# One batch's last tiles in two orders: TensorE's and VectorE's own, two transposes copied by ScalarE, and routing logits computed without a transpose

## The reference, cut to what matters

```python
x = x + attn(layernorm(x))        # 16 heads of 16; rotated scores over a plain-score denominator
x = x + ffn(layernorm(x))
# ffn(x):
out_shared = square(relu(x @ Ws1)) @ Ws2
logits = x @ Wr                                   # 8 experts
top_vals, top_idx = top_k(logits, 2)
prob = trunc(scatter(softmax(top_vals), top_idx)) # is 1 only where one softmax weight rounds to 1
out = out_shared + sum_e prob[e] * (square(relu(x @ W1[e])) @ W2[e])
```

## Time and profile before

| | |
|---|---|
| time, median of 3 runs | 1656.57 us (1656.44 to 1657.23) |
| the profiled execution's own time | 1656.43 us |
| its span | 1654.7 us |
| ScalarE busy | 1587.1 us, 96% of the span |
| TensorE busy | 1483.4 us, 90% |
| last score exponential ends | 1625.3 us; 29 us of the span follow it |

### The profile page before, as it was taken

One profiled execution on the slowest core, in us unless ns is written; L12 is line 12 of the kernel. 1 busy time (PEld: TensorE's weight loads), 2 busy tenths in 40 slices (PEclk: granted clock), 3 DMA queues, 4 the chain that ended last, 5 costly groups with the idle time before them and its releaser, 6 DMA issues.

```text
span 1654.7 us, 25505 instructions
## 1 busy us (share of the span) xinstructions
PE 1483.4 (90%) x8226; PEld 572.7 (35%) x8226; DVE 851.1 (51%) x1961; ACT 1587.1 (96%) x2641; POOL 521.9 (32%) x863
## 2 busy tenths in 40 slices
PE   4888989999999989999899899989999999999986
PEld 2322333333333333333343343333333333333334
DVE  5334434765346653566445653566434665356416
ACT  2999999999999999999999999999999999999992
POOL 3324133432234322333332323334133432234310
PEclk8998999999999999999999999999999999999998
DMA  5532233331434313333234234333243421433300
GB/s 160 156 99 80 86 106 115 120 101 55 131 115 131 111 44 122 122 124 106 80 118 124 94 96 131 100 121 97 73 131 115 141 93 42 135 113 103 115 27 26
DMA packets 95389, 172.05 MB, mean 104 GB/s; under 512 B 15696, under 2 KB 82256, under 8 KB 83152
## 3 DMA queue, kind: packets, MB, share of 16 engines
q1 hardware_dynamic: 94656, 169.55, 32.7%
q10 hardware_dynamic: 592, 0.79, 0.2%
HBM read 111.55 MB, written 58.72 MB: 103 GB/s over the span
## 4 chain that ended last, share of the span: by engine, by line
ACT 88%; PE 6%; issue 4%; DVE 1%; DMA 1%; DVEq 0%; ACTq 0%; POOL 0%; SPq 0%; POOLq 0%
ACT scores L541 57%; ACT probs L551 27%; ACT probs L553 4%; PE scores L599 2%; PE y_ps L628 1%; PE side L638 1%; PE scores L606 1%; PE scores L657 0%; DMA x_in<-in_L_attn_x 0%; PE side L657 0%; PE scores L647 0%; PE scores L773 0%; ACTq L315 0%; PE scores L784 0%; DVEq L894 0%
## 5 line engine op out<-in xcount | busy, mean ns | idle before, releaser
L541 ACT ACTIVATE scores<-scores 128x1024 f32<-128x1024 f32 x1024 | 1067.6, 1122 | 16.8 <-PE scores L599 16.5
L599 PE MATMUL scores<-stack 96*128 96x512 bf16 x2048 | 585.3, 385 | 77.8 <-ACT scores L541 40.1
L551 ACT ACTIVATE probs<-scores 128x1024 f32<-128x1024 f32 x512 | 491.7, 1111 | 2.8 <-PE scores L606 1.7
L606 PE MATMUL scores<-stack 96*128 96x512 bf16 (+3 forms) x1536 | 335.0, 330 | 46.7 <-ACT scores L541 37.6
L438 POOL TENSOR_SCALAR_AFFINE_SELECT probs<-probs 128x256 f32<-128x256 f32 (+1 forms) x640 | 240.8, 403 | 387.7 <-ACT probs L551 219.0
L628 PE MATMUL y_ps<-probs,v_sb 128*32 128x512 f32 (+3 forms) x3072 | 331.8, 504 | 5.1 <-POOL probs L438 5.1
L599 PEld LDWEIGHTS scores<-stack 96*128 96x128 bf16 x2048 | 152.6, 97 | 486.1 <-ACT scores L541 209.9
L541 ACT ACTIVATION_READ_ACCUMULATOR scores<-scores 128x1 f32 x1024 | 300.5, 293 | 0.0
L448 POOL TENSOR_TENSOR parts<-rest,parts 128x512 bf16<-128x512 f32 x124 | 143.2, 1155 | 292.8 <-DVE parts L961 292.8
L606 PEld LDWEIGHTS scores<-stack 96*128 96x128 bf16 x1536 | 116.9, 98 | 300.1 <-ACT scores L541 154.5
L446 POOL TENSOR_TENSOR rot<-raw,cos_sb 128x512 f32<-128x512 f32 x62 | 89.3, 1440 | 390.2 <-DVEq L971 390.2
(11 more groups left out here) (141 smaller groups left out, 1062.0 us busy)
## 6 DMA issues: line engine op xcount, KB each, us to landing
stack<-qk_parts SPq DMA_DIRECT2D x756, 128.0 KB, 2.6
qk_parts<-parts SPq DMA_DIRECT2D x127, 384.0 KB, 2.6
out<-x_mid SPq DMA_DIRECT2D x32, 256.0 KB, 2.9
x_in<-in_L_attn_x SPq DMA_DIRECT2D x7, 1024.0 KB, 5.3
stack<-qk_parts SPq DMA_DIRECT2D x18, 64.0 KB, 2.3
x_in<-in_L_attn_x SPq DMA_DIRECT2D x2, 512.0 KB, 4.4
probs<-in_L_attn_Wqkv SPq DMA_DIRECT2D x1, 512.0 KB, 5.7
cos_sb<-in_cos SPq DMA_DIRECT2D x1, 512.0 KB, 6.5
```

What stands on the lines that cost most here:

```text
L541: nc.scalar.activation(src, src, ACT.Exp, scale=SCALE, accum_out=den[:, g % 2, i, j:j + 1]).then_inc(exp_done, 1)
L551: nc.scalar.activation(probs[:, chunk % 2, j, :], src, ACT.Exp, scale=SCALE).then_inc(exp_done, 1)
L599: mm = nc.tensor.matmul(tile[:, half * HALF:(half + 1) * HALF], q[:, j, i * P:(i + 1) * P], k[:, j, half * HALF:(half + 1) * HALF], start= ...
L606: mm = nc.tensor.matmul(tile[:, col:col + n], k[:, h, i * P:(i + 1) * P], q[:, h, q0:q0 + n], start=True, stop=True)
```

## The change

The list is given in two orders. `END_TILES` is the order in which TensorE fills tiles, `END_READ` the one in which VectorE reads them, and `END_COPIED` names two tiles, ("t2", 0) and ("t2", 1), that ScalarE copies to `xn2t` after its last exponential, with a semaphore of its own, `end_copied`. The tiles logits_t are gone: a logits tile is now 4 blocks times 2 halves of the contraction, with the tokens as the stationary operand (128x128) and the 8 router columns as the moving one, and it waits for both t2 tiles of its half. VectorE's read of it is a plain copy of 32 columns. TensorE's waits name the tile (`end_read`) instead of its number. The routed tile now comes before ("down", 0) and ("down", 1).

```diff
-END_TILES = [("norm", 0), ("acc", 2), ("acc", 3), ("t2", 2), ("t2", 3), ("norm", 1), ("up", 2),
-             ("logits_t", 1), ("acc", 0), ("acc", 1), ("up", 3), ("down", 2), ("t2", 0), ("t2", 1),
-             ("logits", 1), ("down", 3), ("logits_t", 0), ("up", 0), ("up", 1), ("logits", 0), ("down", 0),
-             ("down", 1), ("routed", 0)]
+END_TILES = [("norm", 0), ("acc", 2), ("acc", 3), ("t2", 2), ("t2", 3), ("norm", 1), ("acc", 0), ("acc", 1), ("up", 2),
+             ("up", 3), ("logits", 1), ("t2", 0), ("t2", 1), ("down", 2), ("logits", 0), ("up", 0), ("down", 3), ("up", 1),
+             ("routed", 0), ("down", 0), ("down", 1)]
+END_READ = [("norm", 0), ("acc", 2), ("acc", 3), ("t2", 2), ("t2", 3), ("norm", 1), ("acc", 0), ("acc", 1), ("up", 2),
+            ("up", 3), ("logits", 1), ("down", 2), ("logits", 0), ("up", 0), ("routed", 0), ("down", 3), ("up", 1),
+            ("down", 0), ("down", 1)]
+END_COPIED = [("t2", 0), ("t2", 1)]
...
+            for tile in END_COPIED:
+                n, t = END_TILES.index(tile), tile[1]
+                act.wait_ge(end_full, n + 1)
+                nc.scalar.activation(xn2t[:, :, 2 * t * P:(2 * t + 2) * P], bank(n).rearrange("p (k n) -> p k n", k=KC),
+                                     ACT.Copy).then_inc(end_copied, 1)
             exp_gap(B - 1)
...
+            def end_read(tile):
+
+                if tile in END_COPIED:
+                    pe.wait_ge(end_copied, END_COPIED.index(tile) + 1)
+                else:
+                    pe.wait_ge(end_taken, END_READ.index(tile) + 1)
+
...
-                elif what == "logits_t":
-                    pe.wait_ge(end_taken, END_TILES.index(("t2", 2 * t + 1)) + 1)
-                    for k in range(KC):
-                        for j in range(2):
-                            mm = nc.tensor.matmul(side[32 * j:32 * j + 32, 0:2 * P], wr_sb[:, k, :],
-                                                  xn2t[:, k, (4 * t + 2 * j) * P:(4 * t + 2 * j + 2) * P],
-                                                  start=k == 0, stop=k == KC - 1, tile_position=(0, 32 * j),
-                                                  skip_group_check=True)
                 elif what == "logits":
-                    pe.wait_ge(end_taken, END_TILES.index(("logits_t", t)) + 1)
-                    for i in range(2):
-                        mm = nc.tensor.transpose(side[:, i * P:(i + 1) * P], logits_t[:, i * P:(i + 1) * P], ident[:, :])
+                    end_read(("t2", 2 * t))
+                    end_read(("t2", 2 * t + 1))
+                    for i in range(NB // 2):
+                        for k in range(KC):
+                            mm = nc.tensor.matmul(side[:, i * E:(i + 1) * E], xn2t[:, k, (4 * t + i) * P:(4 * t + i + 1) * P],
+                                                  wr_sb[:, k, 0:E], start=k == 0, stop=k == KC - 1)
...
             for n in range(IN_LOOP, len(END_TILES)):
-                pe.wait_ge(end_taken, n - 2 * RING + 1)
+                if n >= 2 * RING:
+                    end_read(END_TILES[n - 2 * RING])
                 end_tile(n, bank(n))
...
-                elif what == "logits_t":
-                    nc.vector.tensor_copy(logits_t[0:P // 2, :], side[0:P // 2, 0:2 * P]).then_inc(end_taken, 1)
                 elif what == "logits":
                     half = slice(t * NB // 2, (t + 1) * NB // 2)
-                    nc.vector.tensor_copy(logits[:, half, :].rearrange("p (j i) e -> p i j e", i=2),
-                                          side[:, 0:2 * P].rearrange("p (i j e) -> p i j e", i=2, j=4)[:, :, 0:2, 0:E]
+                    nc.vector.tensor_copy(logits[:, half, :].rearrange("p i e -> p (i e)"), side[:, 0:E * NB // 2]
                                           ).then_inc(end_taken, 1)
...
-            for n in range(IN_LOOP, len(END_TILES)):
-                end_tile(n, bank(n))
+            for tile in END_READ[IN_LOOP:]:
+                end_tile(tile, bank(END_TILES.index(tile)))
             experts(last_b)
```

More of the change, by code:

```diff
@@ L276, in block @@
         end_taken = sem("end_taken")
+        end_copied = sem("end_copied")
         raw_of = [raw[:, :], y_sb[:, 0, 0:HALF]]
@@ L758, in end_tile @@
                 elif what == "acc":
-                    pe.wait_ge(end_taken, END_TILES.index(("norm", 1 - t // 2)) + 1)
+                    end_read(("norm", 1 - t // 2))
                     for i in range(2):
@@ L768, in end_tile @@
                                                      xn[:, t % 2, i, k * P:(k + 1) * P], ident[:, :])
-                elif what == "logits_t":
-                    pe.wait_ge(end_taken, END_TILES.index(("t2", 2 * t + 1)) + 1)
-                    for k in range(KC):
-                        for j in range(2):
-                            mm = nc.tensor.matmul(side[32 * j:32 * j + 32, 0:2 * P], wr_sb[:, k, :],
-                                                  xn2t[:, k, (4 * t + 2 * j) * P:(4 * t + 2 * j + 2) * P],
-                                                  start=k == 0, stop=k == KC - 1, tile_position=(0, 32 * j),
-                                                  skip_group_check=True)
-                elif what == "logits":
-                    pe.wait_ge(end_taken, END_TILES.index(("logits_t", t)) + 1)
-                    for i in range(2):
-                        mm = nc.tensor.transpose(side[:, i * P:(i + 1) * P], logits_t[:, i * P:(i + 1) * P], ident[:, :])
+                elif what == "logits":
+                    end_read(("t2", 2 * t))
[4 more added lines that the diff above has]
+                                                  wr_sb[:, k, 0:E], start=k == 0, stop=k == KC - 1)
                 elif what == "up":
-                    pe.wait_ge(end_taken, END_TILES.index(("t2", t)) + 1)
+                    end_read(("t2", t))
                     for k in range(KC):
@@ L1096, in ffn_tile, with end_tile @@
                     dve.drain().then_inc(out_ready, 1)
-            def end_tile(n, side):
-                what, t = END_TILES[n]
+            def end_tile(tile, side):
+                what, t = tile
                 b = B - 1
@@ L1105, in end_tile @@
                     route(b)
-                dve.wait_ge(end_full, n + 1)
+                dve.wait_ge(end_full, END_TILES.index(tile) + 1)
                 if what == "norm":
@@ L1220, in batch @@
                         if kind == "end":
-                            end_tile(t, side)
+                            end_tile(END_READ[t], side)
                         elif kind == "v":
```

## The result

The changed kernel takes 1659.88 us (median of 14 executions, 1656.43 to 1662.79) against 1656.51 of the kernel before on the same chip (14, 1654.41 to 1659.59): a ratio of 1.0022 with a 95% interval of 1.0015 to 1.0029. It is slower by 3.4 us, just over the 0.2% that I had set as the bound, and inside the range; but the forecast was "no change, a shade faster", and it is rival 3's time, 1659.7, that came. The profiled execution took 1659.48 with a span of 1657.9.

A forecast was written before the change was run, and what follows sets the result against it. ScalarE's exponentials bound the kernel (88% of the chain), with a 28.3 us tail at stake. Gains of 2.4 + 0.5 less 2.6 given back left 0.3 us: 1656.3 us, range 1653.7 to 1660.0.

The forecast's parts named there:

- rival 3: Second tail stretch: logits 0's small products don't count as work, clock low to the end; 1659.7 us, chance 0.25.
- the sum: Whole tail: clock low at 1637.70, back 6.0 us after restart; 2.4 + 0.5 gained, 2.6 lost, 0.3 left; chance 0.45.
- rival 2: Second tail stretch: clock stays high after short idle; last add 1649.4, span end 1652.1, time 1654.0 us; chance 0.20.
- the end: After the last add: store issue, landing and SyncE's last wait take 2.7 us; span ends 1654.4 against 1654.7.
- acc ahead: First tail part: acc directly behind norm's read, so the first transpose starts at 1637.70; 2.4 us gained.
- hidden behind VectorE's layernorm: TensorE's up 2, up 3 and logits 1 fit beside VectorE's 5.8 us, ending 1635.5 with 2.2 us to spare.
- one of the two things that were to show me wrong: Signs of error: down 2 waiting for hidden 2, or TensorE waiting for ScalarE's copies; neither was expected.
- the price of a small product: Logits tile: each load with 8 columns starts 0.11 us apart at the high clock, 0.22 at the low.
- The upper end: Small products of the logits tile: whole load with nothing overlapped, 0.19 us at the high clock, 0.333 at the low.
- the second half of rival 3: Logits 0 at the low clock with whole 0.333 us loads: 1.8 us more, 1661.5 us; chance 0.10.
- the copies: ScalarE copies two transposed tiles, 598 ns each, no second table load charged; 0.7 us cover before TensorE needs them.
- The rule that transposes don't count as work for the clock: Second tail stretch: 6.0 us would count from down 2, clock rising at 1645.45; 1656.9 us, chance 0.10; rows spoke against it.

The follow-up runs named there:

- the cut kernel: Changed kernel computing 2 of its 8 batches, compared with the kernel before cut likewise: 469.98 us against 466.31.
- the fillers: Unneeded 256-column identity products in TensorE's idle tail stretches, added to the changed kernel (1651.67 us) and to the kernel before (1652.63 us).
- the fifth profile: Changed kernel unaltered, run once more for a profile of its slower group: profiled execution 1661.28 us, span 1659.7.
- the filled one: Changed kernel plus unneeded products on TensorE (4 ahead of norm, 1 behind it, 6 behind logits 1): 1651.67 us, repeated 1652.25.
- the first profile: Changed kernel as first measured, nothing further altered: profiled execution 1659.48 us, span 1657.9.
- the cut kernel before: Kernel before the change computing only 2 of its 8 batches: 466.31 us.
- the third profile: Changed kernel unaltered, run once more for a profile: profiled execution 1656.21 us, span 1654.6.

## Why the prediction failed

- **The mechanism was on the page, the weight was wrong.** The step that failed is the one that sets the sum: "If the clock is low at 1637.70 ... and comes back 6.0 us after the restart, at 1643.7". It treats the return as something that any work earns after six microseconds, the 16 small products of logits 0 included. In four of the five profiles of the full changed kernel the clock was back 2.7 to 4.0 us after the second restart (tails of 27.9, 28.3, 27.7 and 27.1), in the fifth it was low until 12.9 us after it (32.4), and in the cut kernel for ten microseconds (31.6). With wide products ahead of the small ones it was 6.0 again. The sum's middle case was met by none. What the runs showed in its place: when logits 0 runs at the low clock, the clock stays low for 10.2 to 13.7 us in all, and the tail lasts 31.4 to 32.6 us where the kind case has 27.1 to 28.3. The parts taken singly say that the router tile makes the loss, and the times, of which 18 in 26 lie at 1659.5 or above, that a loss is the usual case: rival 3 had 0.25 and should have weighed most. How it acts is seen in four profiles, two of them with VectorE's copies, and agrees with the fillers, which take the whole loss back.
- **How close rival 3 came is in part luck.** By its sum the tail was to last 32.6 us (1625.2 to 1657.85), and the fifth profile has 32.4; but the last add came 28.9 after the last exponential where the sum has 29.9, and the end behind it took 3.5 where it has 2.7. The kind tails, 27.1 to 28.3, lie nearest to rival 2's (1652.1 - 1625.2 = 26.9), though the clock did fall in them. And the median of 1659.88 is made of both kinds of tail and of exponentials that ended at different times.
- **What I held against rival 3 was no evidence.** "The router tiles before were thin too, 32 rows wide, and the clock rose behind both": thin in rows of the array, but each product streams 256 columns. The new tile's stream 8 behind each load of 128x128. The runs that tell them apart are the old router in the new order (1.0001) and the new router in the old order (1.0020).
- **Right: acc ahead, 2.4 us.** t2 starts 11.31 us after norm, 11.35 forecast; 11.34 in the fifth profile. Right as well: up 2, up 3 and logits 1 are hidden behind VectorE's layernorm (logits 1 ends at 1640.8, xn is ready at 1642.2), and down 2's hidden tile was in time in the full kernel's profiles. In the cut kernel, where the transposes ran at the high clock, down 2 waited 0.23 us for it, one of the two things that were to show me wrong, at a small price.
- **Right: the price of a small product.** 0.11 at the high clock and 0.22 at the low one gave 1.8 and 3.5 for sixteen; measured 1.85 and 3.42. The upper end, the whole load of 0.333 with nothing overlapped, is out, since the loads of logits 0 took 333 ns each and still started 0.21 apart. So the second half of rival 3 is out, too.
- **Right: the copies.** 598 ns each, no second table load, 0.2 us or more ahead of TensorE's need. One of them may still have cost something; their effect on the times stays open, as said.
- **A term off: the end.** "2.7 from the last add": in the five profiles of the changed kernel it took 3.5 (1654.40 to 1657.9), 3.9, 3.2, 2.7 and 3.5, in the filled one 2.7. What varies is SyncE's last wait, which is for the store (SyncE's waits of the changed kernel: line, what for, us in total, times, longest):

```profile
SPq L172 <- DMA out<-x_mid: 2.5, 1, 2.5
```

It was 1.7 in the filled kernel and 2.6 in the fifth profile. I had taken the landing of 2.1 from the issue's start. With 3.5, half a microsecond of "gained" becomes a loss of 0.3; with 2.7, as once in five, it is as worked out.
- **The rule that transposes don't count as work for the clock** (the Trainium skill, TensorE: Matmul & The Clock Gate, Part 4: PE-mode transpose) was set against the rows. In the first profile the clock came back 2.7 us after a restart with 1.9 us of transposes and half of down 2. By the rule it should have come later than without them, so this run speaks against it as the rows did. No run leaves the transposes out, so the rule isn't tested by itself.
- **What stays open: the size of the loss.** The five profiles of the full changed kernel have tails of 28.7 us on average, the two of the kernel before 29.4. By these alone the tail is no slower. Even with the bad tail of 32.4 in every execution it would lose 3.0, and of the three profiled ones at 1658.9 or above only one had it. The other two had late exponentials: the last one ended between 1625.9 and 1630.1 in the five, 1628.0 on average; in the thirteen profiles of the other full kernels between 1622.6 and 1628.2, 1625.4 on average, with the same train. That is 2.6 us apart with a standard error of 1.0. The filled changed kernel, identical up to the last exponential, had 1622.7 and 1625.0, and its mean of 1652.3 less a tail of 25.1 and the 1.7 outside the span leaves 1625.5. So I take the train's difference for chance; it is not shown, nor in how many executions the bad tail occurs.

## What to carry to other kernels

An operation that loads many weights for few columns can be cheap by its duration and dear by its neighbours, as logits 0 was: try it behind wide products or where nobody waits, and price what follows it at both clocks. A serial tail with idle TensorE stretches can be worth filling with unneeded products (4 to 8 us here) before its order is worth tuning. Where times of one kernel spread by more than the effect sought, one profile of each may point the wrong way: compare the same stretch in several.

## What was not expected of the hardware

- The clock fell at 1641.6 although TensorE had been idle for only 0.8 us (logits 1 ended at 1640.8); before the change it held for 3.9 idle microseconds after wide products (1635.4 to 1639.3). The length of the idle time alone does not decide it. What had run before may count, but the profiles are mixed: behind wide products it held for only 2.2 us in the cut kernel before and through 4.7 with the router alone exchanged, behind small ones through 2.5 in the third profile of the changed kernel.
- It can fall in the middle of work: at 450.7 in the cut kernel, as down 2 began, 1.6 us after the restart.
- It can come back 2.7 us after a restart or 12.9 us after it, in the same program on the same data (first and fifth profile). The 6.0 and 6.1 that I had read from one profile are no constant. The two differ by little beforehand: the clock fell 0.7 us ahead of the restart in the first (1641.6, 1642.34) and 0.8 ahead of it in the fifth (1638.9, 1639.65). With 0.7 stand two more profiles of the changed kernel, both back after 2.7 us; with 0.8 to 0.9 the second one with VectorE's copies (12.8) and the one with the wide products first (6.0). So a tenth of a microsecond may part the kind case from the bad one; no run was made to test it.
